# Attention with experts: the last rows' probabilities transposed by VectorE and carried through DRAM, instead of by TensorE

## What is computed

```python
q, k = apply_rope(split_heads(x @ Wq)), apply_rope(split_heads(x @ Wk))
v = split_heads(x @ Wv)
sim = einsum('bid,bjd->bij', q, k) * d ** -0.5
sim = where(tril, sim, -inf)
attn = softmax(sim, axis=-1)
out = einsum('bij,bjd->bid', attn, v) @ Wo + bo
x = layernorm(x + out)
x = layernorm(x + ffn(x))   # top 2 of 8 experts, gelu(x w_up) w_down, weighted
```

## Time and profile before

| | |
|---|---|
| median of 3 runs | 831.53 us (831.14 to 834.18) |
| profiled execution, its own time | 833.04 us |
| its span | 831.3 us |
| busy PE | 808.4 us, 97% |
| busy DVE | 671.6 us, 81% |
| busy ACT | 621.6 us, 75% |
| busy POOL | 391.7 us, 47% |
| moved by DMA | 78.62 MB, mean 95 GB/s |

### The profile page before, as it was taken

The page is one execution under the profiler, slowest core; times in us unless marked ns, Lnnn a source line. Parts: engine busy times, 40 slices in busy tenths (PEclk is TensorE's granted clock), DMA queues, the critical chain, the costliest instruction groups (busy, mean ns, idle before and its releaser), DMA issues.

```text
span 831.3 us, 21041 instructions
## 1 busy us (share of the span) xinstructions
PE 808.4 (97%) x6267; PEld 591.3 (71%) x6267; DVE 671.6 (81%) x2590; ACT 621.6 (75%) x1672; POOL 391.7 (47%) x485
## 2 busy tenths in 40 slices
PE   8999999999999999999999999999999989999996
PEld 4566667666666666666666666666666669999995
DVE  6787798889888988899889988988898866123897
ACT  3677787888788878887788778878877766555577
POOL 3343433225433543343336533543363236989883
PEclk9999999999999999999999999999999999999999
DMA  4322312122322221222222222221123357434525
GB/s 145 121 84 89 109 58 85 62 76 74 102 71 82 75 91 69 78 78 77 77 77 77 78 77 77 77 90 65 68 81 112 113 142 206 129 84 129 159 81 157
DMA packets 75279, 78.62 MB, mean 95 GB/s; under 512 B 10336, under 2 KB 51040, under 8 KB 75168
## 3 DMA queue, kind: packets, MB, share of 16 engines
q1 hardware_dynamic: 70800, 68.42, 25.8%
q0 software_dynamic: 4224, 8.72, 3.1%
q10 hardware_dynamic: 144, 0.13, 0.1%
HBM read 28.39 MB, written 12.14 MB: 49 GB/s over the span
## 4 chain that ended last, share of the span: by engine, by line
PE 90%; DVE 4%; ACT 3%; issue 3%; DMA 1%; another core or an unknown queue 0%; SPq 0%; DVEq 0%; ACTq 0%
PE TB L1036 17%; PE S_all L989 17%; PE TB L1020 14%; PE S_all L1187 8%; PE AO L1057 7%; PE AO L1200 4%; PE TB L1200 4%; PE AO L918 3%; PE AO L916 3%; PE AO L917 3%; PE S_all L1020 2%; ACT PT L1317 2%; PE AO L980 1%; PE AO L979 1%; PE AO L978 1%
## 5 line engine op out<-in xcount | busy, mean ns | idle before, releaser
L1305 ACT ACTIVATE Pr_all<-Sm,nmax 128x512 f32<-128x512 f32 (+3 forms) x512 | 280.6, 554 | 1.4 <-DVE nmax L1520 1.4
L1520 DVE CUSTOM_DVE_ANT_0 Sm<-S_all,causal 128x512 f32<-128x512 f32 (+3 forms) x512 | 220.0, 487 | 67.7 <-PE S_all L989 67.6
L678 POOL TENSOR_TENSOR kT<-shared,kT 128x512 f32<-128x512 f32 x63 | 80.1, 1272 | 314.6 <-DMA kT<-shared 312.6
L1317 ACT ACTIVATE PT<-TB 128x1024 f32<-128x1024 f32 x185 | 131.0, 742 | 63.5 <-PE TB L1020 60.2
L989 PE MATMUL S_all<-kT,qT 64*128 64x512 f32 (+3 forms) x1024 | 166.9, 444 | 2.7 <-DVE nmax L1520 2.1
L1036 PE MATMUL TB<-PT,shared 128*64 128x128 f32 x1008 | 149.8, 438 | 5.3 <-ACT PT L1317 0.3
L1541 DVE SCALAR_TENSOR_TENSOR x_acc<-AO,rinv,x_acc 128x128 f32<-128x128 f32 x504 | 141.7, 344 | 3.9 <-remote 1.5
L1020 PEld LDWEIGHTS TB<-ident,Pr_all 128*128 128x128 f32 x1000 | 108.0, 141 | 38.4 <-ACT Pr_all L1305 21.4
L1020 PE MATMUL TB<-ident,Pr_all 128*128 128x128 f32 x1000 | 133.8, 277 | 0.5 <-ACT PT L1317 0.5
L989 PEld LDWEIGHTS S_all<-kT,qT 64*128 64x128 f32 x1024 | 79.1, 187 | 72.0 <-issue 55.2
L1036 PEld LDWEIGHTS TB<-PT,shared 128*64 128x64 f32 x1008 | 69.3, 136 | 58.0 <-issue 38.6
(11 more groups left out here) (319 smaller groups left out, 1337.5 us busy)
## 6 DMA issues: line engine op xcount, KB each, us to landing
kT<-shared SPq DMA_DIRECT2D x124, 128.0 KB, 2.0
qT<-shared SPq DMA_DIRECT2D x124, 128.0 KB, 2.0
wo<-in_wo SPq DMA_DIRECT2D x64, 64.0 KB, 1.9
PT<-yrows SPq DMA_DIRECT2D x7, 512.0 KB
w_tile<-in_wup SPq DMA_DIRECT2D x10, 256.0 KB
xt<-xrows SPq DMA_DIRECT2D x32, 65.0 KB
x_acc<-in_x SPq DMA_DIRECT2D x8, 256.0 KB
wdown<-in_wdown SPq DMA_DIRECT2D x8, 256.0 KB
```

The source lines that it names most:

```text
L678: nc.gpsimd.tensor_tensor(kT[p][:, :], k_cos, kT[p][:, :], ALU.add).then_inc(k_ready, 1)
L1305: nc.scalar.activation(Pr[j][:, 0:n], Sm[j], ACT.Exp, bias=nmax[:, j:j + 1], scale=-1.0, accum_out=rsum[p][:, h * QB + qb:h * QB + qb + 1] ...
L1317: last = nc.scalar.activation(PT[p][:, :, 0:qb + 1, qb * P:qb * P + P], source, ACT.Copy)
L1520: nc.vector.tensor_tensor_reduce(out=Sm[j], in0=SB[2 * (group % 2) + h][:, at:at + n], in1=causal[:, T - n:T], scale=-0.125, scalar=HUGE, ...
```

## The change

1. **The last 128 rows** (group 0) are no longer transposed by PE, but for the very last unit. `turn` on DVE turns the 128x512 probabilities of each head in 32x32 squares. This leaves each square inside its own 32 partitions, so the squares still have to change partitions: SP stores them to a DRAM scratch (`turns`, one DMA of 512 KB) and loads them back into `PT` (four DMAs of 128 KB, one for each 32 partitions). `PT` has a new layout for this, in strips of 32 columns; `attend` reads strips of 32, and `copy_pt` writes them. `attend` now waits for these loads (`turns_in`).
2. **Keys.** `rope_k`, but for the first two units, leaves DVE: ACT copies the projected keys out of PSUM (`keep_k`), and POOL does both products (`turn_k`). The rotations of POOL move one unit later, and the swaps of q and k become two DMAs of 256 KB.
3. **PE's order.** `project_q` goes ahead of the group 2 transposes, not behind them, and both go into `TB`; `attend` goes into the bank of the keys (`AB`), for which it waits on `keep_k`.
4. ACT does the `exp` of groups 0 and 1 in the unit itself, group 2's in the next.
5. `rope_q` on DVE stands ahead of the batch's norm and routing steps, and `norm_x1` on POOL is one unit later.

```diff
-        PT = [sb(f"PT{i}", [P, 2, QB, T]) for i in range(2)]
+        PT = [sb(f"PT{i}", [P, T // SQ, 2 * QB, SQ]) for i in range(2)]
...
         def q_bank(u):
-            return AB if u == 0 else OB
+            return AB if u == 0 else OB if u == 1 else TB[:, 1, :]
...
         def o_bank(u):
-            return SB[0] if u == UNITS - 2 else TB[:, 0, :]
+            return TB[:, 0, :] if u == UNITS - 1 else AB
...
+            def store_turned(u, p):
+
+                sp.wait_ge(turned, 2 * u + 2)
+                wait(sp, turns_in, LOADED * (u - 1))
+                sp.dma_start(turns[p * P:p * P + P, :], turned_pr[:, :, :, :].rearrange("p b c s -> p (b c s)")).then_inc(stored, 16)
+
+            def load_turned(u, p):
+
+                sp.wait_ge(stored, 16 * (u + 1))
+                wait(sp, pv_done, u - 1)
+                squares = turns[p * P:p * P + P, :].rearrange("(a r) (b n) -> b r a n", r=SQ, b=LANES)
+                for b in range(LANES):
+                    sp.dma_start(PT[p][SQ * b:SQ * b + SQ, LANES * (QB - 1):, :, :].rearrange("k a c s -> k a (c s)"),
+                                 squares[b]).then_inc(turns_in, 16)
...
+            def swap(u, p):
...
+                sp.dma_start(qk[p][0:P:2, :, :], qk_rot[1:P:2, :, :]).then_inc(swapped, 16)
+                sp.dma_start(qk[p][1:P:2, :, :], qk_rot[0:P:2, :, :]).then_inc(swapped, 16)
...
+            def turn_k(u):
+
+                pool.wait_ge(k_kept, u - PLAIN + 1)
+                nc.gpsimd.tensor_tensor(k_rot, k_cos, sin_t[:, :], ALU.mult)
+                nc.gpsimd.tensor_tensor(k_cos, k_cos, cos_t[:, :], ALU.mult).then_inc(k_read, 1)
...
+                if PLAIN <= u + 1 < UNITS:
+                    rotate_k(u + 1, 1 - p)
+                    rotate_q(u + 1, 1 - p)
                 if u + 2 < UNITS:
-                    rotate_k(u + 2, p)
-                    rotate_q(u + 2, p)
+                    turn_k(u + 2)
...
+                pe.wait_ge(turns_in, LOADED * (u + 1))
+                if u < UNITS - 1:
+                    pe.wait_ge(k_kept, min(u + 2, UNITS - PLAIN))
...
+                        to = o_bank(u)[D * h:D * h + D, kb * P:T].rearrange("d (t s) -> d t s", s=SQ)
+                        last = nc.tensor.matmul(to, V[u // VS % 2][:, kb, u % VS * P + D * h:u % VS * P + D * h + D],
+                                                pt_rows(p, h, kb), start=(kb == QB - 1), stop=(kb == 0),
...
+            def keep_k(u):
+                act.wait_ge(k_proj, u + 1)
+                act.wait_ge(k_ready, u)
+                nc.scalar.activation(k_cos, k_bank(u), ACT.Copy).then_inc(k_kept, 1)
...
+            def turn(u, h):
+
+                dve.wait_ge(exped, BLK * u + h + 1)
+                wait(dve, stored, 16 * u)
+                nc.vector.transpose(turned_pr[:, :, h:2 * QB:2, :].rearrange("p b k s -> p k b s"),
+                                    Pr[h].rearrange("p (k b s) -> p k b s", b=LANES, s=SQ)).then_inc(turned, 1)
...
-                for j in range(2, BLK):
+                for j in range(FIRST_OF[1], FIRST_OF[2]):
                     mask_max(u, j)
+                if not last:
+                    for h in range(2):
+                        turn(u, h)
+                for j in range(FIRST_OF[2], BLK):
+                    mask_max(u, j)
+                if not first and u + 2 < UNITS:
+                    rope_q(u + 2)
```

More of the change, by code:

```diff
@@ L3 @@
 from contextlib import ExitStack
+from itertools import accumulate
 F32 = mybir.dt.float32
@@ L30 @@
 SWAPPED = 2 * 16
+SQ = 32
+LANES = P // SQ
+LOADED = LANES * 16
 VS = 4
@@ L145, in sb, with in_turn @@
             return ctx.enter_context(nc.sbuf_tensor(name, shape, dtype))
+        def in_turn(first, then):
+            with ExitStack() as attention_only:
+                held = [attention_only.enter_context(nc.sbuf_tensor(*of)) for of in first]
+            return held, sb(*then)
         def ps(name, shape=(P, 512)):
@@ L179, in build_block @@
         wo = [sb(f"wo{i}", [P, C]) for i in range(2)]
-        qT = [sb(f"qT{i}", [P, T]) for i in range(2)]
-        kT = [sb(f"kT{i}", [P, T]) for i in range(2)]
+        qk = [sb(f"qk{i}", [P, 2, T]) for i in range(2)]
+        qT, kT = ([qk[i][:, which, :] for i in range(2)] for which in range(2))
         shared = sb("shared", [P, 3 * QB * VS * P + PAIRS * P])
@@ L192, in build_block @@
         Sm = [Sm_of[qb][:, h, :] for h, qb in ORDER]
-        Pr_all = sb("Pr_all", [P, BLK, T])
-        Pr = [Pr_all[:, i, :] for i in range(BLK)]
+        (Pr_all, turned_pr), f_acc = in_turn(
+            [("Pr_all", [P, QB * (QB + 1) * P], F32), ("turned_pr", [P, LANES, 2 * QB, SQ], F32)], ("f_acc", [P, NT, C], F32))
+        ends = list(accumulate((qb + 1) * P for h, qb in ORDER))
+        Pr = [Pr_all[:, end - (qb + 1) * P:end] for end, (h, qb) in zip(ends, ORDER)]
         nmax = sb("nmax", [P, BLK])
@@ L307, in o_bank, with turn_banks, turn_blocks, pt_block_rows @@
         def o_bank(u):
-            return SB[0] if u == UNITS - 2 else TB[:, 0, :]
+            return TB[:, 0, :] if u == UNITS - 1 else AB
         def y_bank(u):
             return (SB[2], SB[3]) if u == UNITS - 1 else (AB, OB)
-        def wide(u):
-            return S_all[:, 0:2, :] if u == UNITS - 1 else AO if u >= UNITS - 3 else TB
+        def turn_banks(u, group):
+            two = TB if u < UNITS - 1 or group == 0 else S_all[:, 2 * group - 2:2 * group, :]
+            return two.rearrange("k b n -> k (b n)")
+        def turn_blocks(group):
+            return [(qb, [(h, kb) for kb in range(qb + 1) for h in range(2)]) for qb in GROUPS[group]]
+        def pt_block_rows(p, qb):
+            return PT[p][:, LANES * qb:LANES * qb + LANES, 0:2 * qb + 2, :].rearrange("k a c s -> k c a s")
+        def pt_rows(p, h, kb):
+            return PT[p][:, LANES * kb:, 2 * kb + h, :]
         XB, HB, FB = [AB[:, 0:P], TB[:, 1, 0:P]], SB[0:3], [OB[:, 0:C], TB[:, 0, 0:C]]
@@ L821, in attention @@
                     send_row(batch - 2, 2 * n - 1)
-                if batch > 0 and n == NORM_AT:
+                if batch > 0 and n == NORM_AT + 1:
                     norm_x1(batch - 1)
@@ L1160, in attention @@
                     turn_places(0, batch - 1, u)
-                if not first:
-                    transpose(u - 1, 1 - p, 2)
-                if u + 2 < UNITS:
-                    project_q(u + 2, *second)
                 if not first:
@@ L1299, in exp @@
                 act.wait_ge(maxed, g + 1)
-                if j == FIRST_OF[group]:
-                    wait(act, transposed, 3 * (u - 1) + group + 1)
+                if group == 0:
+                    wait(act, turned, 2 * (u - 1) + j + 1)
+                elif j == FIRST_OF[group]:
+                    wait(act, transposed, 2 * (u - 1) + group)
                 if j == 0:
@@ L1764, in attention @@
                 mask_max(u, 1)
-                if u < 2:
-                    (rope_k, rope_q)[u](u + 1)
+                if u == 0:
+                    second_k()
+                if u == 1:
+                    rope_q(2)
                 if u >= 2:
                     scale_y(u - 2)
-                for j in range(2, BLK):
+                for j in range(FIRST_OF[1], FIRST_OF[2]):
                     mask_max(u, j)
+                if not last:
+                    for h in range(2):
+                        turn(u, h)
+                for j in range(FIRST_OF[2], BLK):
+                    mask_max(u, j)
+                if not first and u + 2 < UNITS:
+                    rope_q(u + 2)
                 if u == 1:
@@ L1803, in attention @@
                     place_rows(batch - 1)
-                if u + 2 < UNITS:
-                    rope_k(u + 2)
-                    if not first:
-                        rope_q(u + 2)
                 if not first:
@@ L2108 @@
     args.append(nc.dram_tensor("yrows", (Y0 + B * T * K, C), F32, kind="Internal").ap())
+    args.append(nc.dram_tensor("turns", (2 * P, 2 * T), F32, kind="Internal").ap())
     out = nc.dram_tensor("out_0", (B * T, C), F32, kind="ExternalOutput").ap()
```

164 lines of the change are left out of this document (74 added, 90 removed).

## The result

| | before | after |
|---|---|---|
| median, runs on one chip | 831.8 us (831.14 to 834.18, 4 runs) | 809.93 us (809.43 to 812.21, 4 runs) |
| ratio, 95% interval | | 0.9737 (0.9711 to 0.9764) |
| profiled execution, its own time, span | 833.04, 831.3 us | 809.77, 808.0 us |
| moved by DMA | 78.62 MB | 144.66 MB |

What follows compares the result with a forecast made beforehand. Attention was taken as bound by TensorE, VectorE not far behind. A unit of 9.38 + 0.20 = 9.58 us against 10.33 gave 0.75 x 60 = 45, less 2: 43 us, so 831.5 - 43 = 788 us; range 773 to 836.

Steps and rivals of the forecast that it cites:

- Transposes off TensorE, -0.85: TensorE, each unit: the last rows' transposes leave the bounding engine, so all 0.85 us counts.
- Queries ahead, -0.35 + 0.25: TensorE before attending: wait for the 1024-column copy goes (-0.35 us), new wait for group 2's copy comes (+0.25).
- Plain unit 9.24: TensorE's plain unit falls from 10.19 us to 9.24; with 0.14 for the routing, 9.38.
- VectorE's unevenness +0.20 a unit: Three heavy VectorE units of eight (norm, root, tables): 0.4 to 0.65 us waiting each, 1.6 per batch, +0.20 per unit.
- Turn 0.62: VectorE: each turn taken as 0.62 us from the shuffle, 1.24 for both, not slowed by GpSimd.
- Strips cost nothing: Attending's reads and ScalarE's copies in strips of 32 columns: no added time.
- The store lands in 4.0, the loads in 2.0, squares hidden by 1.3 us: SP's queue: store lands in 4.0 us, last load in 2.0; rows there at 15.0, needed at 16.3.
- In the last units ... I add 2 us in all: Last units: the store stands behind expert weight loads that wait for the unit's maxima; 2 us in all.
- That cover goes in one unit of eight, by up to 1 us, and falls in a heavy unit, where TensorE waits anyway: GpSimd: norm of four tiles ahead of the rotation ScalarE's key copy needs; up to 1 us, while TensorE waits anyway.
- I expect its granted clock to stay at 1.00: TensorE: with waits of some 0.4 us of a unit, granted clock stays at 1.00, the 2.4 GHz level.
- 512 transposes fewer: Sign that would show the forecast: 512 fewer transposes on TensorE.
- The third (late squares): Rival: turned squares land 0.7 to 1.0 us late, TensorE stands some 0.5 per unit; 818 us; chance 0.14.

Runs made afterwards that it cites:

- e7: Changed kernel with the eight transposes of the 1024-column group done twice on TensorE in every unit; 844.30 us, ratio 1.0160 to the kernel before.
- e10: Changed kernel with TensorE's query projection put back behind the last group's transposes; 813.68 us, ratio 0.9774 to the kernel before.
- e6: Changed kernel with VectorE's turns left out from unit 2 on, old turned rows used; 800.49 us, ratio 0.9646 to the kernel before.
- e1: Changed kernel with SyncE's first expert weight loads (units 58 to 62) behind the unit's store and turned-row loads; 802.38 us, ratio 0.9653 to the kernel before.
- e11: Kernel of e5 with the front's sums halved into units 45 and 46, and unit 0's turned-row loads ahead of the queries' swap; 795.97 us, ratio 0.9566.
- e5: Kernel of e1 with the swaps of keys and queries taken apart, keys first; 795.61 us, ratio 0.9578 to the kernel before.

## Why the prediction was off

- *Transposes off TensorE, -0.85*: right. 0.87 (e7).
- *Queries ahead, -0.35 + 0.25*: the sum was nearly right, its parts not. The wait of 0.35 goes in either order, and the order itself costs 0.10 in a plain unit (e10: 9.17 against 9.27), by a wait inside attending of 0.11 (2.41 against 2.30, start to start) and not 0.25. In return the last four transposes take 0.53 until attending starts (231.50 to 232.03), where the sum had 0.35.
- *Plain unit 9.24*: 9.27. *VectorE's unevenness +0.20 a unit*, 1.6 a batch: 0.9 to 1.3 (e6). Together with the routing a unit was to take 9.58, 76.6 a batch; units 33 to 41 took 76.65. That this agrees to the tenth is in part luck: late rows are in the 76.65 and not in the sum.
- *Turn 0.62*: right; two take 1.30, the mask pass behind them starts 1.22 after the first, beside GpSimd's passes too. The Trainium skill (SBUF — State Buffer, Who interferes with whom) says that a VectorE instruction with one SBUF input, outside the two-port modes, does not contend with GpSimd; the trace agrees: 119 of the 126 turns ran mostly beside a GpSimd pass and took 688 ns on average, the other seven 691.
- *Strips cost nothing*: attending is 2.30 us where nothing waits, as before; the copies of 1024 columns take 1.08 or 1.09 us (1.09 before). Right.
- *The store lands in 4.0, the loads in 2.0, squares hidden by 1.3 us*: half right. The two errors (2.7 and 3.6 in the median) nearly cancel, but 1.3 us was no cover for loads that take up to 4.6: the rows are 0.6 us ahead in the median, and in twelve units attending starts right at their landing, up to 0.5 us late.
- ***"In the last units ... I add 2 us in all"*: the step that failed most, 11.5 instead of 2.** (The 11.5 are of one execution; e1, which takes this step away, gives 7.0 by the medians.) The mechanism was named, its price was not worked out: the weights' load waits for the end of `attend`, so the store goes 6 us late, lands in 6.0, and TensorE stands 4.00 once, with a lower clock behind it. I had taken a cost for a queue without asking how long the instruction ahead waits.
- ***"That cover goes in one unit of eight, by up to 1 us, and falls in a heavy unit, where TensorE waits anyway"*: the second, 7.3 in units 41 to 45.** I counted GpSimd's mean (7.1 of 9.6), and the norm, but neither the small sums of the front (4.2 us beside the norm's 3.2) nor that the keys' copy, and so `attend`, hangs on the end of all this. A cover of 7.04 us had become one of 3.0.
- *Not in the sum at all*: the start, 2.8 us (the loads of unit 0 stand behind a swap that goes at 24.44, and nothing covers the rows for the first attending, which starts at 30.79 instead of 28.06; in e11 it starts at 28.08); VectorE passes with both operands in SBUF beside a busier GpSimd (2.11 and 3.3 instead of 0.17 in units 43 and 44; rows 8 had been read for the turns alone); and the ring of swap, rotations and products, which has 0.6 us to spare in a plain unit. e5 gave 6.2 us for a keys' swap that no longer waits for the queries.
- *"I expect its granted clock to stay at 1.00"*: true of plain stretches (1.00 over 200 to 300), wrong behind its stands: after 1.75 and 1.35 us of them (to 438.33 and 440.34) 0.50 over 440 to 446.
- *"512 transposes fewer"*: 504, since the very last unit keeps its eight.

None of the rivals came about at its price. The third (late squares) happened in part: in the last units by the queue's order, and in twelve others by loads slower than forecast.

## What to carry to other kernels

A plain step with many small parts can be forecast to the tenth of a microsecond and the total gain still come out at half, because what is lost lies in the few units that are unlike the others: go through the first, the last, and each one with extra work on any engine, one by one, before multiplying. When work moves to an engine that was idle half its time, the question is not its new mean load but which of its instructions has a due time, and how much stands between it and its release in the worst unit. A cover has to be set against the spread of what it covers, not its median. In an in-order queue, a transfer that others now wait for must not stand behind one that waits for a late event, and two transfers with different due times should not be made one.
